# A two-layer adaLN/attention/MoE/fp8-MLP kernel: second layer's MLP without the products of zeros on TensorE

## What is computed

```python
def _reorder_quantize_x(x, idx):
    scale = jnp.max(jnp.abs(x)) / GLOBAL_DIV
    xr = (x / scale)[:, idx]
    scale_x = jnp.max(jnp.abs(xr), axis=1, keepdims=True) / FP8_MAX
    return (_fp8(xr / scale_x), scale_x, scale)
...
qx, sx, sc = _reorder_quantize_x(xf, up_reorder_index)      # 1024 rows of 256
g = _qlinear(qx, sx, sc, w_gate, up_reorder_index, out_idx=down_reorder_index)
u = _qlinear(qx, sx, sc, w_up, up_reorder_index, out_idx=down_reorder_index)
t = jax.nn.silu(g) * u                                      # 1024 rows of 704
qt, st, sct = _reorder_quantize_x(t, down_reorder_index)
y = _qlinear(qt, st, sct, w_down, down_reorder_index)
```

## Time and profile before

| | |
|---|---|
| median of 3 runs | 648.83 us (648.53 to 650.09) |
| the profiled execution's own time | 650.63 us |
| its span, first to last instruction | 648.5 us |
| PE busy | 503.3 us, 78% |
| DVE busy | 518.6 us, 80% |
| ACT busy | 359.1 us, 55% |
| POOL busy | 262.1 us, 40% |
| mean granted TensorE clock | 0.953 |

### The profile page before, as it was taken

One profiled execution on the slowest core, in us unless ns is written; L12 is line 12 of the kernel. 1 busy time (PEld: TensorE's weight loads), 2 busy tenths in 40 slices (PEclk: granted clock), 3 DMA queues, 4 the chain that ended last, 5 costly groups with the idle time before them and its releaser, 6 DMA issues.

```text
span 648.5 us, 10885 instructions
## 1 busy us (share of the span) xinstructions
PE 503.3 (78%) x3862; PEld 411.0 (63%) x3862; DVE 518.6 (80%) x973; ACT 359.1 (55%) x760; POOL 262.1 (40%) x212
## 2 busy tenths in 40 slices
PE   2011198599999999998578997979988999666775
PEld 1000043278888878887458896979978999533453
DVE  4999868688888888885528958998889889579993
ACT  3226235687777778775115545645455456447671
POOL 3565114754444445530554279361362140070011
PEclk9999999989999999999579999999998999978797
DMA  8300004050000000000278796779875764030001
GB/s 269 118 0 1 1 1 129 0 172 2 1 2 3 1 2 10 25 1 3 77 252 327 273 312 142 259 269 254 294 285 166 285 147 132 27 103 25 9 25 33
DMA packets 36529, 71.85 MB, mean 111 GB/s; under 512 B 5276, under 2 KB 21916, under 8 KB 36220
## 3 DMA queue, kind: packets, MB, share of 16 engines
q10 hardware_dynamic: 16912, 46.27, 21.0%
q1 hardware_dynamic: 16491, 16.75, 8.1%
q0 software_dynamic: 3072, 8.14, 5.2%
HBM read 66.03 MB, written 5.12 MB: 110 GB/s over the span
## 4 chain that ended last, share of the span: by engine, by line
PE 49%; DVE 32%; issue 7%; ACT 6%; POOL 2%; DMA 1%; ACTq 0%; DVEq 0%; SPq 0%; POOLq 0%; PEldq 0%
PE pw L418 8%; PE pb L418 8%; PE pb L609 7%; PE sc L609 6%; PE sc L459 6%; PE po L418 4%; PE pt L470 3%; DVE areg L1168 2%; DVE areg L1154 2%; DVE areg L1152 2%; DVE rs L1566 1%; DVE areg L1513 1%; DVE areg L1165 1%; DVE areg L1506 1%; DVE breg L1225 1%
## 5 line engine op out<-in xcount | busy, mean ns | idle before, releaser
L609 PE MATMUL pb<-areg,wreg 128*128 128x128 f32 x736 | 86.3, 275 | 6.1 <-DVE areg L1506 3.8
L609 PEld LDWEIGHTS pb<-areg,wreg 128*128 128x128 f32 x736 | 84.0, 192 | 7.2 <-issue 5.2
L609 PE MATMUL sc<-areg,wreg 128*128 128x128 f32 x552 | 67.5, 280 | 8.7 <-DVE areg L1506 8.7
L1711 POOL TENSOR_TENSOR breg<-breg,con 128x512 f32<-128x512 f32 x32 | 40.7, 1271 | 80.9 <-ACT breg L846 80.9
L609 PEld LDWEIGHTS sc<-areg,wreg 128*128 128x128 f32 x552 | 65.3, 196 | 9.5 <-DVE areg L1506 9.5
L418 PE MATMUL pb<-areg,wreg 128*128 128x512 f16 x240 | 58.9, 382 | 2.0 <-ACT breg L846 1.9
L980 ACT CAST areg<-areg 128x512 f16<-128x512 f32 (+1 forms) x46 | 25.8, 561 | 62.5 <-DVE areg L1506 56.0
L418 PE MATMUL pw<-areg 128*128 128x256 f16 x406 | 56.5, 273 | 1.6 <-DVE areg L1520 1.6
L854 ACT ACTIVATE breg<-breg,mx 128x128 f32<-128x128 f32 (+1 forms) x128 | 56.6, 445 | 2.0 <-DVE mx L1276 1.9
L459 PE MATMUL sc<-areg,breg 128*128 128x128 f32 (+1 forms) x256 | 48.0, 331 | 6.4 <-DVE mx L1276 5.2
L1520 DVE TENSOR_TENSOR areg<-areg 128x512 f16<-128x512 f32 (+1 forms) x46 | 39.8, 866 | 14.0 <-ACT areg L980 13.7
(11 more groups left out here) (245 smaller groups left out, 1246.7 us busy)
## 6 DMA issues: line engine op xcount, KB each, us to landing
wreg<-in_L_ffn_w ACTq DMA_DIRECT2D x46, 896.0 KB, 7.3
wreg<-in_L_ffn_w SPq DMA_DIRECT2D x8, 896.0 KB, 7.8
ys_dram<-areg ACTq DMA_DIRECT2D x23, 128.0 KB
wreg<-in_L_ffn_wq SPq DMA_DIRECT2D x1, 2048.0 KB, 8.6
wreg<-in_L_ffn_wo SPq DMA_DIRECT2D x1, 2048.0 KB, 8.1
areg<-in_fside_BxSxS ACTq DMA_DIRECT2D x4, 256.0 KB, 5.5
x_in<-in_x SPq DMA_DIRECT2D x4, 256.0 KB, 4.0
h_dram<-areg SPq DMA_DIRECT2D x8, 128.0 KB, 1.7
```

What stands on the lines that cost most here:

```text
L609: last = nc.tensor.matmul(bank[:, j * P:(j + 1) * P], up_w[n % SLOTS_UP][:, m, c, at:at + P], xsT[:, parity, c * P:(c + 1) * P], start=c = ...
L1711: G.tensor_tensor(t2[:, parity, :].rearrange("p (b n) -> p b n", b=2), t2[:, parity, :].rearrange("p (b n) -> p b n", b=2), rope_sin.rearr ...
```

## The change

All calls of `keep_clock` in the second layer are taken out: 10 products before the first transposes, 10 before and 16 after the first inner transposes, 2 at the end of each of the five loop iterations, 3 and 4 in the tail, 53 products in all. No other instruction, wait or order is touched; nothing waits on these products and they signal nothing.

```diff
@@ -707,16 +707,13 @@
             pe.wait_ge(s["fold_low"], 2)
             pe.wait_ge(s["inner_low"], 2 * MT)
             pe.wait_ge(s["x1_ready"], 1)
-            keep_clock(pt2[:, 1, :], 10)
             quantised_transposes(0)
             gate_products(0)
             quantised_transposes(1)
             up_products(0)
             gate_products(1)
             up_products(1)
-            keep_clock(pt2[:, 1, :], 10)
             inner_transposes(0)
-            keep_clock(pt2[:, 1, :], 16)
             quantised_transposes(2)
             gate_products(2)
             up_products(2)
@@ -728,13 +725,10 @@
                     quantised_transposes(i + 1)
                 inner_transposes(i - 2)
                 down_quantised(i - 3)
-                keep_clock(pt2[:, 1, :], 2)
             inner_transposes(NT - 2)
             down_quantised(NT - 3)
-            keep_clock(pt2[:, 1, :], 3)
             down_quantised(NT - 2)
             inner_transposes(NT - 1)
-            keep_clock(pt2[:, 1, :], 4)
             down_quantised(NT - 1)
```

## The result

Beside the kernel before on one chip, the changed kernel took 653.61 us (652.70 to 654.51), the kernel before 649.46 (646.95 to 650.78). The ratio is 1.0066, interval 1.0042 to 1.0089: the change costs 0.4 to 0.9% of the time, some 4 us. The profiled execution took 654.22 us with a span of 652.1, against 650.63 and 648.5 before, so 3.6 us more. Forecast were 2.5 us more, and 651.3 as the time. The direction was right, the amount was too small.

What follows compares the result with a forecast made beforehand. DVE was taken to bound the second layer's MLP, with zeros mattering through the clock. Terms 0.8 + 0 + 0.9 - 0.4 + 1.2 = +2.5 us on the median 648.83 gave 651.3 us, range 648.2 to 653.7.

Steps and rivals of the forecast that it cites:

- First call: Ten zeros before tile 0: without them its up products run largely at half clock, +0.8 us, bounds +0.1 and +1.1.
- Third call: Sixteen zeros before tile 2's transposes: without them tile 2 meets the half level, +0.9 us, bounds 0.4 and 1.4.
- Second call: Ten zeros ahead of the first inner transposes: removal costs nothing, covered by a 3.09 us wait for DVE.
- The loop: Two zeros in each of five iterations: removal ends DVE's wait at tile 4, -0.4 us; nothing at the late end.
- The tail: Three and four zeros: without them last inner transposes and last down products run at half level, +1.2 us; otherwise 0 or -0.8.
- The quick clock: Rival: any work restores the clock as fast as zeros, 3.4 us after real work begins everywhere; 648.1 us, chance 0.15.
- the tail needs no zeros: Rival: in the tail the clock is back at 639.2 as now, the rest as forecast; +1.3, 650.1 us, chance 0.15.
- a fall in the loop: Rival: without zeros the clock falls once in the loop too, DVE waits 2.4 us more; 653.7 us, chance 0.15.

Runs made afterwards that it cites:

- the first call back: Changed kernel with the ten products of zeros ahead of tile 0's transposes put back; 652.17 us, ratio 1.0044 to the kernel before.
- the third: Changed kernel with the sixteen products of zeros after the first inner transposes put back; 652.36 us, ratio 1.0048 to the kernel before.
- the tail's: Changed kernel with the tail's two calls, three and four products of zeros, put back; 650.91 us, ratio 1.0032 to the kernel before.
- the moved call: Kernel before with the third call's sixteen zeros moved ahead of the first inner transposes, twenty-six in a row there; 650.59 us, ratio 1.0029.
- the placed zeros: Kernel before without second call and loop zeros; fourteen added ahead of tile 4's transposes and of tile 6's inner transposes, nine instead of three in the tail; 647.82 us.
- hardly a pause: Placed zeros plus tile 7's inner transposes ahead of tile 6's down products, then zeros in nearly every second-layer wait; 646.48 us, ratio 0.9963 to the kernel before.

## Why the prediction was off

*What bounds, and through what.* Right. DVE is the bound (16.15 of 17.00 us), the zeros cost nothing in their waits (TensorE stood still for another 0.25, 3.09 and 1.44 us behind those of the first three calls), and the loss comes through the clock at tile 0, tile 2 and in the tail. DVE's waits account for the whole difference. What failed is the size of two terms: the 3.75 us along DVE, where 2.5 were forecast, lie just beyond the 3.7 to which the bounds add up.

*First call, +0.8, bounds 0.1 and 1.1.* Too small: 1.19 at tile 0, and 0.20 more at tile 1, 1.39 together. The step that failed is the choice inside the bounds, and the late bound itself: the clock was back 6.6 us after TensorE took up work (575.2 to 581.8), beyond the 6.3 that I used as the late end, so that the gate products of tile 1 began slowly too, a part that I had not counted.

*Third call, +0.9, bounds 0.4 and 1.4.* Too small: 1.69. I put it in the middle because its products run without a pause, as the zeros do, and took the 3.4 us for half of the case. The lag was 5.8 us, and both groups ran slowly nearly to the end; the late bound was 0.2 to 0.3 short, since slow transposes and the copy delay the gate products by another 0.1 (0.86 us behind the transposes, not 0.75) and each group takes 2.33 from start to start with 0.2 us of run-out behind the second.

How far a middle between 3.4 and 6.3 was from what real work got at these two tiles, seven cases without zeros show: 6.6 and 5.8 us in the changed kernel, 5.9 with the first call back (tile 2), 5.9 with the third (tile 0), 5.8 and 5.3 with the tail's (tiles 0 and 2), 6.1 with the moved call (tile 2). None is below 5.3. In all of them the clock had been at half level for 4 us or more before TensorE took up the work. The row from which I had the early end is another case: there the clock fell at 588.0, just as TensorE took up work, and was back 3.4 us later.

Tile 4 shows both cases with real work alone. The first three lines are from the changed kernel, the others from that with the third call back:

```profile
608.55 0.29 PE L660 MATMUL po<-identb,areg 128*128 128x128 f16 x2 [3.14 <-DVE areg L1569]
609.14 1.91 PE L702 MATMUL pw<-areg 88*128 88x256 f16 x8
612.86 1.36 PE L668 MATMUL pb<-w_up,areg 128*128 128x352 f16 x8
...
606.70 0.40 PE L660 MATMUL po<-identb,areg 128*128 128x128 f16 x2 [3.90 <-DVE areg L1570]
609.44 2.55 PE L668 MATMUL sc<-x_in,areg 128*128 128x352 f16 x8
611.79 1.39 PE L668 MATMUL pb<-w_up,areg 128*128 128x352 f16 x8
```

In the changed kernel the clock fell at 609.1, when TensorE was already at work, and was back at 612.5, 4.0 us after TensorE had begun. With the third call back it had been at half level since 605.0 and was back at 611.85, 5.15 us after TensorE had begun. So the short lag is not the zeros' alone, but in these last 80 us no start without zeros had it at a clock that had been at half for 1.7 us or more (5.15 us or more passed). Zeros at such a start did better: ahead of tile 0 they had the clock back 3.1 to 4.5 us after the first of them, in six profiles; with the third call back it took 5.7, the transposes before the zeros included (589.1 to 594.8). Whether zeros are quicker because they run without a pause or because of what they are, no run here separates.

*Second call, 0.* Right: without it, in the kernel with the placed zeros, tile 2 stands at 29.59 as before.

*The loop, -0.4.* Right in the profiles: -0.48, -0.47, -0.48. The case that I had reckoned with, half level from the start of the chain, is that of the kernel with the third call back, and DVE's wait at tile 4 is gone there too. What was missing is that the same removal lengthens the pause ahead of tile 3's inner transposes from 0.55 to 2.32 us, and 1.2 to 1.3 us behind this pause the clock fell in two of the profiles. In the changed kernel's profile it did not.

*The tail, +1.2.* Right: +1.15, with 1.87 and 1.89 us for the last two groups of down products and the clock at half level to the end. The spread that I gave it (down to -0.8) is real, but on the other side: with these zeros the tail takes 13.50, 12.58, 12.57 or 13.87 us in four profiles, without them 14.65 or 14.66 in three. That the number fits to 0.1 us is therefore partly luck, that of the execution of before that was profiled; against the others the loss is 0.8 to 2.1 us.

*The sum.* 1.39 + 1.69 - 0.48 + 1.15 = 3.75 measured, against 0.8 + 0.9 - 0.4 + 1.2 = 2.5. Two of four terms are right to 0.1 us, two were mis-sized by 0.6 and 0.8. The timed 4.15 us lie above the profile's 3.6, within the interval.

*The rivals.* The quick clock did not occur at tile 0, at tile 2 or in the tail. That the tail needs no zeros is refuted by the kernel with them put back. The trace of the changed kernel does not show a fall in the loop (1.00 from 613 to 632 us); that of the placed zeros does, once, at a price of 0.37 us and not the 2.4 that I had worked out. My price left out that TensorE is ahead of DVE there: without a fall the up products of tile 6 end at 624.38 in the changed kernel, 1.4 us before DVE takes them at 625.78; and with the placed zeros the clock was back in the second of the slow groups (at 622.3 us, a group of 1.71 us after one of 2.55).

## What to carry to other kernels

Products of zeros that look like waste can pay for the clock of the few products on which the bounding engine waits, as these 53 did, without which the kernel takes some 4 us more: before taking them out, find for each the next real product that someone waits for, and price that at the half level (2.53 us for a group that takes 1.37 at full), with the lag that real work has needed in the trace after a clock long at half level (5.3 to 6.6 us at tiles 0 and 2), not the one of zeros (3.1 to 4.5 us ahead of tile 0) or of a clock that has only just fallen (4.0 us at tile 4 of the changed kernel). Here the place of the zeros counted and not their number: with all of them kept, but 6.51 us of standing still before tile 2, its groups of products took 2.53 us each. Zeros belong into waits, and should end just before the wait does: in the kernel with hardly a pause, where they do, TensorE stands still for at most 0.88 us at a time in its work on the eight tiles, and the clock reads 1.00 to its last product. An engine's waits, stage by stage against a common start, give the price of each place in the profiled execution to some 0.1 us, where whole times scatter by 3 us (647.69 to 650.74 in 29 runs of the kernel before); look where that execution stands among the others before taking its price for the median's.

## What the hardware showed that I had not expected

With the first call back the clock came back and fell again within 3.4 us although TensorE worked in between (back at 574.7, fallen at 578.1, with the gate products between them and a wait of 1.4 us). The same pause of 2.32 us in the loop was followed by a fall in two profiled executions and by none in four others. So one profile of such a kernel shows one of several outcomes; with TensorE at work nearly throughout, six runs lay within 0.8 us, where six of the kernel before lie within some 2.3.
